# A fused attention, liquid-scan and expert kernel: a further order of all five engines, and 24 weight loads on ScalarE's queue

## What is computed

```python
x = x + scan(cond_attention(x, attn_bias, mask))
x = x + experts(cond2_attention(x, ones_mask))

def cond_attention(x):        # 16 heads of 64, one shared key/value head
    xn = layernorm(x, g_in)
    q, (k, v) = xn @ Wq / 8, split(xn @ Wkv)
    k, v = [null_k; k], [null_v; v]
    return layernorm(softmax(masked(q k^T + bias)) v @ Wo, g_out)

def scan(x):                  # EXPAND 2: 512 channels, 16 states
    x_in, z = split(rmsnorm(x) @ in_proj)
    x_in = silu(x_in)
    a, b, c = sigmoid(x_in @ A_proj + bias), x_in @ B_proj, x_in @ C_proj
    h_t = a_t * sigmoid(A_base) * h_(t-1) + b_t x_t ;  y_t = h_t . c_t
    return x + ((y + D * x_in) * silu(z)) @ out_proj

def cond2_attention(x):       # as the first, with q and k normed to length 1, scale 8,
    ...                       # and a bias that a small network computes from positions
def experts(x):               # the expert of the largest gate logit, of 8
    return onehot(argmax(x @ gate_w + gate_b)) . (x @ expert_w + expert_b)
```

## Time and profile before

| | |
|---|---|
| median of 3 runs | 1658.18 us |
| lowest and highest | 1657.03, 1659.58 us |
| the profiled execution | 1662.17 us |
| its span in the trace | 1660.3 us |
| mean granted clock of TensorE | 0.963 |
| busy: TensorE, VectorE, ScalarE, GpSimd | 1483.6 (89%), 1142.1 (69%), 1028.1 (62%), 860.0 us (52%) |
| bytes moved | 28.24 MB, mean 17 GB/s |

### The profile page before, as it was taken

How to read it: one execution, slowest core, us unless ns; L and a number is a source line. 1 busy time by engine, 2 the same in 40 slices (tenths; PEclk the granted TensorE clock), 3 DMA queues, 4 the chain that set the end, 5 groups by cost and what they waited for, 6 DMA issues and landing times.

```text
span 1660.3 us, 37684 instructions
## 1 busy us (share of the span) xinstructions
PE 1483.6 (89%) x13903; PEld 1172.8 (71%) x13903; DVE 1142.1 (69%) x2622; ACT 1028.1 (62%) x2431; POOL 860.0 (52%) x552
## 2 busy tenths in 40 slices
...
GB/s 225 99 8 8 2 11 11 11 6 8 11 11 11 12 11 11 11 6 8 11 11 11 11 11 11 11 5 8 12 11 11 11 11 12 8 5 4 8 4 7
DMA packets 40378, 28.24 MB, mean 17 GB/s; under 512 B 19826, under 2 KB 38402, under 8 KB 40196
## 3 DMA queue, kind: packets, MB, share of 16 engines
...
...
## 4 chain that ended last, share of the span: by engine, by line
DVE 35%; PE 24%; issue 15%; POOL 13%; ACT 8%; DVEq 1%; POOLq 0%; ACTq 0%
PE bank L744 7%; POOL c_prob L1648 4%; POOL c_prob L1657 4%; PE bank L734 2%; DVE a_xn L1228 2%; DVE a_prob L1297 2%; PE bank L721 2%; DVE c_c L1462 2%; DVE a_sum L1303 2%; PE bank L709 2%; DVE c_mx L1285 2%; DVE c_sum L1303 2%; PE bank L634 2%; ACT c_prob L995 2%; ACT Ef L1116 2%
## 5 line engine op out<-in xcount | busy, mean ns | idle before, releaser
L1663 POOL TENSOR_TENSOR a_prob<-a_prob,a_rden 128x1024 f32<-128x1024 f32 x32 | 62.8, 1963 | 330.3 <-DVE a_rden L1308 330.3
L1696 POOL TENSOR_TENSOR y<-y,u 128x512 f32<-128x512 f32 x128 | 165.7, 1295 | 21.8 <-DVE u L1402 11.0
L1116 ACT ACTIVATE Ef<-bank 64x512 f32<-64x512 f32 x256 | 150.6, 588 | 4.7
L1688 POOL TENSOR_TENSOR u<-xe,Ef 128x512 f32<-128x512 f32 x96 | 132.7, 1396 | 38.0 <-ACT Ef L1116 38.0
L1643 POOL TENSOR_TENSOR c_prob<-c_qT 128x1024 f32<-128x1024 f32 x32 | 60.6, 1893 | 162.5 <-ACT c_qT L970 162.5
L680 PE MATMUL bank<-a_xnT,a_wq 128*128 128x128 f32 x1024 | 129.7, 281 | 0.3 <-DVE c_prob L1278 0.3
L680 PEld LDWEIGHTS bank<-a_xnT,a_wq 128*128 128x128 f32 x1024 | 123.5, 194 | 6.0 <-DVE c_prob L1278 0.5
L1285 DVE TENSOR_REDUCE c_mx<-c_prob 128x16 f32<-128x1024 f32 x32 | 39.0, 1220 | 126.7 <-POOL c_prob L1657 126.7
L744 PE MATMUL bank<-c_wo,c_prob 128*128 128x256 f32 x512 | 119.7, 387 | 4.4 <-ACT c_prob L1010 4.4
L680 PE MATMUL bank<-c_xnT,c_wq 128*128 128x128 f32 x1024 | 122.8, 278 | 0.0
L1657 POOL TENSOR_TENSOR a_prob<-a_prob,a_mask 128x1024 f32<-128x1024 f32 x32 | 75.9, 2371 | 83.7 <-DVE a_prob L1274 83.7
...
## 6 DMA issues: line engine op xcount, KB each, us to landing
...
```

The lines of the kernel that those rows point to most:

```text
L1116: act.activation(Ef[l][seq, :], src, ACT.Exp, scale=-1.0).then_inc(a.done(f"E{l}{b}"), 1)
L1688: pool.tensor_tensor(u[l][:, :], xi[:, :], (E0u if l == 0 else Ef[l])[:, :], ALU.mult)\
L1696: pool.tensor_tensor(y[:, :], y[:, :], tm[l][:, :], ALU.add).then_inc(g.done(f"y{l}"), 1)
```

## The change

**The loads.** 24 loads leave `load_weights` and are issued by ScalarE on its own queue, in a new function `load_scan_weights`, the first thing that ScalarE's setup does: norm_w, the four pieces of in_proj, four of A_proj, B_proj, C_proj, out_proj, the two of the A bias, D, A_base, and the eight of the position network. Their order among each other, their destinations and their semaphores are the same.

**The order.** `ORDER` and `TURNS` are replaced by others for all five engines. The steps are the same, and so are their inputs and the number of iterations; what differs is the place of the steps in an iteration, the tile that one works on there, and the banks. The cycle is also cut at another place: where TensorE's iteration began with a.PT0, six steps (b.a1, c.xt, c.ex1, c.kv, c.q0, c.q1) that stood near its end now open it with a lag one higher. The setup stays ahead of the same iterations by number, so other steps now lie ahead of or behind it.

```diff
 ORDER = {
     "pe": """
-        a.PT0@2 a.PT1@2 b.gt@3 c.S@4 c.qs@4 b.E0@3 b.E2@3 c.qt@4 a.O@2 a.kv@1 a.q0@1 b.E1@3 b.E3@3 c.oT@5
...
+        b.a1@3 c.xt@4 c.ex1@5 c.kv@4 c.q0@4 c.q1@4 a.PT0@2 c.kT@4 a.PT1@2 c.oT@5 b.gt@3 c.S@4 c.qs@4 c.qt@4
...
 TURNS = {
...
+        c.kT@4>dve.K1 c.S1@4>dve.S1 b.E2@3>act.E30 c.PT1@4>act.PT1 c.O1@4>act.O11 b.z@2>dve.zi""",
...
@@ load_weights, SP
-                load(sp, ld_b, norm_w[:, :], col(ins["L0_attn_norm_w"]))
-                for k in range(KD):
-                    for n in range(2):
-                        load(sp, ld_b, w_in_staged[k][n],
-                             ins["L0_attn_in_proj_w"][k * P:(k + 1) * P, n * E2:(n + 1) * E2])
...
                 load_x(1, ahead=True)
...
-                load(sp, ld_b, w_out[:, :, :], ins["L0_attn_out_proj_w"].rearrange("(k p) n -> p k n", p=P))
...
-                load(sp, ld_mlp, m_w2, ins["L0_cond2_w2"].rearrange("(k p) n -> p k n", p=P))
...
@@ ScalarE
+            def load_scan_weights():
+                load(act, ld_b, norm_w[:, :], col(ins["L0_attn_norm_w"]))
...
+                load(act, ld_b, w_out[:, :, :], ins["L0_attn_out_proj_w"].rearrange("(k p) n -> p k n", p=P))
+                act.wait_ge(zeroed, 1)
...
+                load(act, ld_mlp, m_w1, ins["L0_cond2_w1"].rearrange("(k p) n -> p k n", p=P))
+                load(act, ld_mlp, m_w2, ins["L0_cond2_w2"].rearrange("(k p) n -> p k n", p=P))
+
             def setup_a():
+                load_scan_weights()
                 act.wait_ge(ld_a, n_ld[ld_a.name])
                 act.wait_ge(prep_a, 1)
```

More of the change, by code:

```diff
@@ L108 @@
     "pe": """
-        a.PT0@2 a.PT1@2 b.gt@3 c.S@4 c.qs@4 b.E0@3 b.E2@3 c.qt@4 a.O@2 a.kv@1 a.q0@1 b.E1@3 b.E3@3 c.oT@5
-        c.ex2@5 a.W@2 a.q1@1 c.ex3@5 b.G@3 a.S@1 c.PT0@4 c.PT1@4 b.m0@3 b.xt@2 c.O@4 b.m1@3 c.eb@5 b.x@2
-        c.W@4 b.z@2 a.xt@0 c.ct@4 b.yT@3 b.xiT@2 c.lg@4 c.ex0@4 b.out@3 b.a0@2 b.a1@2 c.xt@3 c.ex1@4 c.kv@3
-        c.q0@3 c.q1@3 c.kT@3""",
+        b.a1@3 c.xt@4 c.ex1@5 c.kv@4 c.q0@4 c.q1@4 a.PT0@2 c.kT@4 a.PT1@2 c.oT@5 b.gt@3 c.S@4 c.qs@4 c.qt@4
+        a.kv@1 a.O@2 b.E0@3 c.ex2@5 b.E1@3 b.E2@3 b.E3@3 a.q0@1 a.W@2 b.G@3 a.q1@1 b.m0@3 c.ex3@5 c.PT0@4
@@ L113 @@
+        c.PT1@4 a.S@1 b.xt@2 c.O@4 b.m1@3 c.eb@5 b.x@2 c.W@4 b.z@2 b.yT@3 b.xiT@2 a.xt@0 c.ct@4 b.out@3
+        c.lg@4 c.ex0@4 b.a0@2""",
     "act": """
[L114 to L117, removed]
+        b.ae0@3 c.xnT@4 b.zs@3 b.ae1@3 c.ksq@4 c.kr@4 c.q0@4 c.q1@4 a.PT0@2 a.PT1@2 b.nl@3 c.oT@5 c.qr@4
@@ L118 @@
+        b.BT@3 a.O0@2 a.O1@2 b.E2@3 b.E3@3 b.E0@3 b.E1@3 c.expm@4 c.prob@4 a.rstd@0 a.q0@1 a.rstd2@2 a.q1@1
+        b.rms@2 c.PT0@4 c.PT1@4 b.xnT@2 c.O0@4 c.O1@4 b.xe@2 b.xs@2 c.rstd2@4 a.expm@1 b.yT@3 b.ze@2 c.cT@4
+        b.xiT@2 a.prob@1 c.le@4 c.rstd@3 a.xnT@0""",
     "dve": """
-        b.xi@3 c.c@5 c.cl@5 b.zg@3 a.sub@2 c.lg@5 b.xl@3 a.st@0 c.oh@5 c.ac0@5 b.x1@4 c.st@4 c.xn@4 a.den@2
-        b.ag@3 b.zi@3 a.xn@0 c.ac1@5 c.ac2@5 b.BC@3 c.ks@4 b.nh@3 a.mk@1 c.V@4 c.mk@4 c.ac3@5 c.K@4 c.qs@4
@@ L121 @@
-        c.S0@4 c.S1@4 a.K@1 a.V@1 c.mx@4 c.sub@4 c.ac4@5 a.st2@2 c.den@4 c.ac5@5 c.ac6@5 a.c@2 c.ac7@5
-        b.Gm@3 b.xn@2 a.S0@1 a.S1@1 b.t1@3 b.yl@2 b.t0@3 b.t3@3 b.t2@3 c.out@5 b.xg@2 a.mx@1 c.st2@4""",
+        c.cl@5 b.xl@3 b.zg@3 c.lg@5 c.oh@5 c.ac0@5 b.x1@4 c.st@4 c.xn@4 a.den@2 c.mk@4 c.ac1@5 c.ac2@5
+        b.BC@3 b.ag@3 b.zi@3 c.ac3@5 c.ks@4 c.K@4 a.st@0 c.V@4 c.qs@4 b.nh@3 c.S0@4 c.S1@4 a.K@1 a.V@1
+        a.mk@1 c.ac4@5 c.ac5@5 c.mx@4 c.sub@4 a.st2@2 b.Gm@3 c.den@4 a.c@2 b.t1@3 b.t0@3 b.xn@2 a.S0@1
@@ L123 @@
+        a.S1@1 c.ac6@5 b.yl@2 b.t2@3 c.ac7@5 b.t3@3 b.xg@2 a.mx@1 c.out@5 c.st2@4 b.xi@2 a.xn@0 c.c@4
+        a.sub@1""",
     "pool": """
-        b.y@3 a.norm@1 c.qsq@3 b.resid@2 b.dx@2 c.addb@3 c.addm@3 b.u0@2 b.u2@2 b.u1@2 c.norm@3 b.u3@2
-        a.addm@0 b.y0@2 b.y1@2 b.y2@2 b.y3@2""",
+        b.u1@4 b.u0@4 c.norm@5 b.u3@4 b.y0@4 b.y1@4 a.addm@2 b.y2@4 b.y3@4 b.y@4 a.norm@2 b.dx@3 c.qsq@4
+        b.resid@3 c.addb@4 c.addm@4 b.u2@3""",
     "sp": """
-        a.mask@1 b.xres@3 a.x@0 c.mask@3 c.store@5""",
+        a.mask@1 a.x@0 c.store@5 c.mask@2 b.xres@2""",
```

47 lines of the change are left out of this document (24 added, 23 removed).

## The result

| | us | runs |
|---|---|---|
| before | 1657.62 (1655.03 to 1659.58) | 8 |
| after | 1662.25 (1659.20 to 1668.30) | 8 |

The ratio is 1.0039, with a 95% interval of 1.0027 to 1.0050: 0.39% slower, 6.5 us by the ratio. The forecast was 1671 against 1658, 0.77% slower. The sign was right, the size half.

What follows compares the result with a forecast made beforehand. It took TensorE's own queue plus its waits as the bound (45.10 us busy of a 46.71 us period). Middle +23, fill -6 and drain -4 made +13 on 1662.2: 1675, or 1671 for the median, range 1640 to 1690.

Steps and rivals of the forecast that it cites:

- loads (a): Start: 24 loads moved to ScalarE's queue save 0.57 us at most; sharing transfers priced at 0, bounds -0.57 to +4.
- middle: Steady periods: new wait of 2.3 us replaces waits of 1.31; +0.8 a period, 29 periods, +23 us (0 to +38).
- (b): Fill: a.sub and a.prob of tile 0 and a.xn of tile 1 ahead of the setup, net -1.3 us.
- (c): Fill: GpSimd's c_bias fold leaves the path between y3 and y of tile 0, -4.7 us (-2 to -7).
- drain: Last iterations: b.m0 runs inside TensorE's wait at c.PT0, twice -2 us, in sum -4 (0 to -6).
- The chain: From a.PT0 through scores, a.O, ScalarE's copies and Ef pieces and GpSimd's u1, u0 to b.m0, at 18.3 us.
- the stretch: TensorE from a.PT0 to b.m0: 16.0 us of its own work in the new order, 20.01 before.
- The wait of 2.3 in the stretch: TensorE's waiting between a.PT0 and b.m0, which it reaches after 16.0 us if unstopped but can start at 18.3.
- the 1.48: Time from c.kT to the scores c.S behind it, 1.48 us, the time of VectorE's K.
- rival 3: "In between": the period grows by about 0.3 and the edges pay it back, 1658 us; 15%.
- The covers hold and b.m0 does not wait: Middle: u0 and u1 ready in time, period 45.7, total 1619 us; 8%.
- The port: a.xn, moved onto the path to c.ct, meets GpSimd's adds; TensorE waits 0.6 more a period, 1688 us; 10%.

Runs made afterwards that it cites:

- e1: Kernel before, with only the 24 loads moved to ScalarE's queue: 1667.93 us, 0.64% slower.
- e8: Kernel before, its order and loads on SP kept, with the three setups placed as in the new order: 1646.68 us, ratio 0.9944.
- e9: Kernel before, with only GpSimd's fold of c_bias moved ahead of the second tile's a.addm: 1650.32 us, ratio 0.9964.
- e3: Changed kernel, with ScalarE issuing its 24 loads only after the first attention's weights have landed: 1658.59 us, ratio 1.0014 to the kernel before.
- e2: Changed kernel with the 24 loads back on SP's queue, so only the order is new: 1654.20 us, 0.25% faster than before.
- e5: New order with loads on SP, and c.ex3 ahead of b.m0 on TensorE: 1653.52 us, ratio 0.9974 to the kernel before.
- e4: Changed kernel with ScalarE's E0 first, GpSimd's u pieces reordered, banks of E1 and E3 exchanged: 1678.15 us, 1.26% slower than before.
- e7: New order, loads on SP, ScalarE's pieces as E0, E2, E1, E3, GpSimd's u0 first, banks of E2 and E3 exchanged: 1691.15 us, 2.07% slower than before.
- e10: Old order with the new setup places, and b.m0 ahead of c.PT0 on TensorE from the 34th iteration on: 1648.64 us, ratio 0.9952.

## Why the prediction was right or wrong

| term | forecast, us | measured, us |
|---|---|---|
| loads (a) | 0 (-0.57 to +4) | +10.6 (e1) |
| middle | +23 (0 to +38) | +6 (traces: 0.2 x 29) |
| fill (b), (c) | -6 | -9 (e8), of which the fold -6 (e9) |
| drain | -4 (0 to -6) | about -1 (what the rest leaves), not told from 0 |
| sum | +13 | +6.5 (the ratio) |

**The loads: wrong.** The step that failed is the sentence "I price that at 0, bounded by +4 (a wait grown by two fifths)". The wait doubled, 10.41 to 20.63. I had seen that the issue time was all that could be saved, and that it was awaited for 0.57 us at most; the price of the other side was then a guess between two bounds, and 0 was taken for no reason in the rows. The Trainium skill, "DMA: Bandwidth & Descriptors", "Issuing engines are not separate DMA queues", was cited there with the right sign, and e1 to e3 agree with it: the DMA engines, busy 84% of the time between 5 and 10 us before (1.05 after), serve both queues at once, and what is needed first is finished later. Half of the longer wait, 5.0 of 10.2 us, came through SyncE's later issue, which the sum had no term for. A second error hid in the first: the profile was of one execution, in which chance had put VectorE's folds beside GpSimd's, and a start at 21.5 was taken for the kernel's.

**The middle: mechanism right, size wrong.** The chain was drawn link by link, and the trace lets each be compared, from a.PT0 (623.64) on: a.O at 5.5 for 5.7; ScalarE's first copy at 6.6 (630.25) for 6.9; its last Ef piece ends at 15.05 (638.69) for 15.5; u1 and u0 end at 17.6 (641.25) for 18.2; b.m0 at 17.9 for 18.3. These are the rows:

```profile
630.25 2.68 ACT L989 ACTIVATE a_prob<-bank,nv_col 64x512 f32<-64x512 f32 x4
632.83 2.42 ACT L1095 ACTIVATE Ef<-bank 64x512 f32<-64x512 f32 x4
...
637.49 1.20 ACT L1095 ACTIVATE Ef<-bank 64x512 f32<-64x512 f32 x2
...
638.83 1.04 ACT L974 ACTIVATE c_prob<-c_prob 128x1024 f32<-128x1024 f32 x1
...
638.76 1.26 POOL L1691 TENSOR_TENSOR u<-xe,Ef 128x512 f32<-128x512 f32 x1 [2.17 <-ACT Ef L1095]
639.98 1.27 POOL L1691 TENSOR_TENSOR u<-xe,u 128x512 f32<-128x512 f32 x1
```

Each link is within 0.3 of its forecast, and the sum of the stretch is 0.45 short of it. That is 2.5% of 17.9 us, and more than half of the forecast of 0.8. The other 0.15 lies in the rest of the period (29.05 for 29.2), and there two errors cancel. The sum left TensorE's own work at its old 45.1 us a period, without a reason, and it fell by 0.7, all of it in this rest (the stretch's own 16.0 came out); and waits of 0.6 came in that the sum did not have, 0.29 for yn and 0.32 at c.W for ScalarE's copies. So that the rest came out within 0.15 is luck. The wait of 2.3 in the stretch came as 1.9: 1.00 at b.m0, 0.51 at the norms' transpose (forecast 0.5), and 0.39 at c.S for the keys, which I had inside the 1.48. With 29 repetitions, a term that is the difference of two chains of 18 us has to be given the error of the chains: +0.8 with bounds of 0 and +1.3 was such a range, and the truth lay in its lower part, where I had put no weight of my own but rival 3, "In between": a period longer by about 0.3 that the edges pay back. e2 is that case (period +0.2, 0.25% faster).

**Rivals.** "The covers hold and b.m0 does not wait" (1619) is refuted by the trace, and e5 shows that it could not have helped: with b.m0's wait gone, two others take its place. "The port" went the other way for a.xn (1.39 before, 0.40 after in the mean), but struck other instructions of VectorE: a_mask from 0.20 to 1.67, a_c from 0.86 to 1.74, yT from 0.37 to 1.03, xe from 0.67 to 1.31. VectorE's busy time in the 1308 us rose from 963 to 1044, and of that only the 0.3 that TensorE waits for yn shows among its waits. The Trainium skill's rule ("SBUF — State Buffer", "Who interferes with whom"), by which also a tensor_tensor with both inputs in SBUF contends with a GpSimd instruction that reads SBUF, agrees with all of these (a_c is such a one, the other three are of the form tensor_scalar), and e4 and e7 show it on the critical path.

**The fill: mechanism right.** The fold's 4.39 us were on the path and left it; e9 puts it at 6.0, with 4.4 inside its interval. (The sum had 4.7 for it, 0.3 more than its rows.) Term (b), -1.3: from TensorE's start to a.PT0 of tile 0 it is 53.3 to 54.7 us in the three traces with the old place of the setup (before, e1, e9) and 52.4 to 53.8 in the five with the new one (after, e2, e3, e8, e10), 1.2 less in the mean. **The drain: wrong.** The step is "b.m0, ready by then, now runs inside the wait". It was not ready: in the changed kernel TensorE waits 4.16 and 7.92 for u0, and then comes to c.PT0 without a wait, so that the wait only moved. In the old order (e10) b.m0's third input, Gm, was the late one, which I had not followed.

What stays open is why one kernel's times spread by some 8 us. Two pairs of traces show where such a difference can lie. From the last b.m0 that waits 1.0 (at 1485.97 in the changed kernel, 1476.47 in e2) to the end both kernels do the same 967 products: in 171.6 us at a mean granted clock of 0.88 in the first, in 178.9 at 0.84 in the second. So those two traces differ by 9.5 us up to there, near e1's 10.6, and by 2.2 at the end. e8 and e10 have the same fill, and there the difference lies in it: e8 starts 2.7 later and is 6.2 behind at the last of the steady b.m0. What makes the clock or the fill differ from one execution to the next is not shown.
